# Second attention of a two-layer block: plain FP32 scores on 32 rows a head, in four row groups, for split scores on 64 rows that went by DRAM

## What is computed

```python
x = L0_attn_x
xn = _layernorm(x, axis=-1)
s = _L0_attn_ref(xn, ...); g = _silu(_L0_ffn_ref(xn, ...)); x = x + s * g
xn = _layernorm(x, axis=-1)
s = _L1_attn_ref(xn, ...)      # below
g = _silu(_L1_ffn_ref(xn, ...))
x = x + s * g

# _L1_attn_ref, HEADS = 16, HEAD_DIM = 16
Q, K, V = X @ Wq + bq, X @ Wk + bk, X @ Wv + bv
...
scores = jnp.einsum('bhqd,bhkd->bhqk', q, k) / np.sqrt(HEAD_DIM)
attn = jax.nn.softmax(scores, axis=-1)
out = jnp.einsum('bhqk,bhkd->bhqd', attn, v)
out = out.transpose(0, 3, 2, 1).reshape(b, s, HEADS * HEAD_DIM)
return out @ Wo + bo
# _L1_ffn_ref: gelu(x16 @ W0.T + bias0) in float16, then @ W1.T + bias1
```

## Time and profile before

| | |
|---|---|
| median of 3 runs | 925.28 us (924.87 to 926.04) |
| the profiled execution | 921.1 us, of which the span is 919.2 us |
| mean granted clock of TensorE | 0.955 of full speed |
| busy share of the span: TensorE, VectorE, ScalarE, GpSimd | 86%, 67%, 51%, 34% |

### The profile page before, as it was taken

One profiled execution on the slowest core, in us unless ns is written; L12 is line 12 of the kernel. 1 busy time (PEld: TensorE's weight loads), 2 busy tenths in 40 slices (PEclk: granted clock), 3 DMA queues, 4 the chain that ended last, 5 costly groups with the idle time before them and its releaser, 6 DMA issues.

```text
span 919.2 us, 13147 instructions
## 1 busy us (share of the span) xinstructions
PE 793.2 (86%) x4544; PEld 480.1 (52%) x4544; DVE 620.4 (67%) x1653; ACT 466.7 (51%) x948; POOL 313.8 (34%) x264
## 2 busy tenths in 40 slices
PE   3556497787999999997999999997999999987996
PEld 1334265673533666773533666773533666763533
DVE  3886757763985677673985677764986577753972
ACT  4456355423367667322467676232477676232464
POOL 0582857200200788200201888200201888100201
PEclk9876789899999999998999999999999999998999
DMA  7311001208300311008300311018200310018200
GB/s 238 114 31 36 23 1 47 75 0 214 86 1 13 94 52 31 1 22 215 63 3 19 88 52 30 1 42 214 45 3 25 81 30 1 1 39 213 49 3 23
DMA packets 54001, 53.25 MB, mean 58 GB/s; under 512 B 14512, under 2 KB 43568, under 8 KB 53936
## 3 DMA queue, kind: packets, MB, share of 16 engines
q1 hardware_dynamic: 51488, 49.70, 20.4%
q10 hardware_dynamic: 2128, 1.68, 0.6%
q0 software_dynamic: 320, 1.05, 0.4%
HBM read 39.00 MB, written 13.14 MB: 57 GB/s over the span
## 4 chain that ended last, share of the span: by engine, by line
PE 56%; DVE 11%; issue 9%; ACT 8%; POOL 7%; DMA 4%; SPq 3%; POOLq 0%; DVEq 0%; ACTq 0%
PE bank L882 9%; PE bank L987 6%; PE bank L976 5%; PE bank L916 5%; PE bank L1153 5%; PE bank L1141 5%; PE bank L1094 4%; PE bank L1126 3%; PE bank L1048 3%; DVE mx L1493 3%; POOL region L567 3%; PE bank L926 2%; PE bank L1131 2%; PE bank L1080 2%; PE bank L958 2%
## 5 line engine op out<-in xcount | busy, mean ns | idle before, releaser
L1493 DVE TENSOR_REDUCE mx<-bank 128x1 f32<-128x512 f32 x256 | 162.9, 683 | 78.8 <-PE bank L1094 77.8
L882 PE MATMUL bank<-xnT,wrope 128*128 128x512 f32 x320 | 151.1, 615 | 18.5 <-ACT region L712 10.4
L567 POOL TENSOR_TENSOR region<-region 128x512 f32<-128x512 f32 x80 | 106.2, 1327 | 175.4 <-DVE region L1328 170.7
L822 ACT ACTIVATE region<-bank 128x512 f32<-128x512 f32 x256 | 136.3, 597 | 52.5 <-PE bank L1131 48.9
L729 ACT ACTIVATE region<-region,nb 128x128 f32<-128x128 f32 x256 | 81.6, 390 | 97.9 <-DVE nb L1335 97.7
L600 POOL TENSOR_TENSOR region<-region,bo_bc 128x256 f32<-128x256 f32 x16 | 11.7, 729 | 289.0 <-DVE region L1384 289.0
L882 PEld LDWEIGHTS bank<-xnT,wrope 128*128 128x128 f32 x320 | 59.6, 197 | 81.2 <-issue 72.1
L1094 PE MATMUL bank<-Kp,Qp 64*128 64x512 f32 x256 | 68.1, 450 | 23.9 <-DMA Kp<-scratch 20.1
L563 POOL TENSOR_TENSOR region<-region,sin_sb 128x512 f32<-128x512 f32 x60 | 80.4, 1340 | 24.5 <-ACT region L712 23.9
L916 PE MATMUL bank<-region 128*128 128x128 f32 x512 | 75.8, 294 | 11.3 <-ACT region L724 9.7
L1321 DVE TENSOR_TENSOR region<-bank,cos_sb 128x512 f32<-128x512 f32 x80 | 54.7, 688 | 43.5 <-PE bank L882 43.3
(11 more groups left out here) (135 smaller groups left out, 1345.3 us busy)
## 6 DMA issues: line engine op xcount, KB each, us to landing
wrope<-in_wrope SPq DMA_DIRECT2D x80, 128.0 KB, 2.1
scratch<-region SPq DMA_DIRECT2D x32, 256.0 KB, 3.8
Qp<-scratch SPq DMA_DIRECT2D x64, 128.0 KB, 3.7
Kp<-scratch SPq DMA_DIRECT2D x64, 128.0 KB, 3.9
X<-in_x SPq DMA_DIRECT2D x4, 512.0 KB, 4.0
scratch<-region SPq DMA_DIRECT2D x16, 128.0 KB, 3.3
out<-X SPq DMA_DIRECT2D x16, 128.0 KB, 2.0
VW<-v_rows SPq DMA_DIRECT2D x16, 102.0 KB, 2.8
```

Source lines behind the costliest of these rows:

```text
L567: nc.gpsimd.tensor_tensor(dst, dst, tiles(sw[:, r % 2, :], i), ALU.add)\
L822: nc.scalar.activation(P1[:, n % 8, :], turned_bank(n)[:, :], ACT.Exp, scale=SCALE1)\
L882: mm = nc.tensor.matmul(misc(b, name)[:, 0:width], lhs(c), xnT[:, c, :], start=(c == 0), stop=(c == DC - 1))
L1493: nc.vector.tensor_reduce(mx1[:, g % 2, column:column + 1], s_ring[m % 3][:, :], AX.X, ALU.max)\
```

## The change

A head gets 32 rows: its 16 dimensions, and 16 rows of which the first is 1 in `Kp` and the negated maximum in `Qp`. The scores are plain FP32, nothing is split, and nothing goes by DRAM: `queries` on ScalarE and `keys` on VectorE write Q and K from PSUM to their rows, once for the even and once for the odd groups, with `own_rows` (1 or 0 for each row) as a factor. Four heads fill the four row groups of 32. The maxima's rows go into `Qp` itself, so the second matmul of a turned tile is gone. The lead holds 7 groups of 4 scores tiles over 4 banks, with one up job behind each (two behind the last); the down projections move to the main loop and the wide part, in portions of 4 to 12 matmuls (`DOWN_STEPS`, by pairs of turned tiles `q`). `down` and `mt` share one bank. In the main loop the four row groups of a half step are those of its two turned and its two scores tiles. `ffn_rows`, `gate_of` and the tanh move with the down projections.

```diff
-HALF = 4 * HD
-NPAIR = NH // 2
+ROWS = 2 * HD
 LEAD = 4 * GH + 12
 WIDE_FROM = 4 * NH - LEAD
-N_SPILL, N_DEAL = 6, 8
-UP_FIRST, DOWN_FROM, DOWN_STEP = 6, 3, 9
+QUADS = LEAD // GH
+UP_PER_QUAD = (1, 1, 1, 1, 1, 1, 2)
+MT_QUAD = 5
+DOWN_STEPS = {0: (0, 12), 1: (0, 12), **{q: (1, 4) for q in range(3, 9)}, **{q: (2, 4) for q in range(11, 17)},
+              **{q: (3, 8) for q in range(20, 26, 2)}}
...
-    jobs += [("dup", i) for i in range(HC)] + [("down", 0), ("down", 1), ("mt", 0), ("down", 2), ("down", 3)]
-    jobs += [("mt", g) for g in range(1, NG)]
+    jobs += [("dup", i) for i in range(MT_QUAD + 1)] + [("mt", 0)] + [("dup", i) for i in range(MT_QUAD + 1, HC)]
+    jobs += [("down", 0)] + [(kind, t) for t in range(1, TT) for kind in ("mt", "down")]
...
-PLACED = {"xh": (0,), "qk": (1, 2, 3, 4), "v1": (5, 6), "dup": (1, 2, 3, 4), "down": (3, 4, 1, 2), "mt": (2,)}
+PLACED = {"xh": (0,), "qk": (1, 2, 3, 4), "v1": (5, 6), "dup": (3, 4), "down": (2,), "mt": (2,)}
...
+TANHS = (7, 21, 37, 54)
+FFN_ROWS, GATES = (33, 47, 62), (38, 53)
...
+        s_quad = s_bank + m_bank[0:2]
+
+        def scores_bank(m):
+            return s_quad[m % 4] if m < LEAD else s_ring[(m - LEAD) % 3]
+
+        def scores_tile(m):
+
+            g, p, par = m // (4 * GH), m % (4 * GH) // 2, m % 2
+            return g, 2 * (1 - p % 2) + par, p // 2
 
         def turned_bank(n):
 
             if n < WIDE_FROM:
                 return t_ring[n % 3]
             k = (n - WIDE_FROM) % 6
-            return t_ring[k] if k < 3 else s_ring[(4 * NH - 6 + k) % 3]
+            return (t_ring + s_ring)[k]
...
-            def spill(b, half): ...
-            def deal(b, g): ...
             def max_rows(b, g):
 
...
-                for part, done in enumerate((mrhi_ready, mrlo_ready)):
...
+                sp.wait_ge(mr_ready.sem, mr_ready.at(b, g + 1))
+                for h in range(GH):
+                    row = h * ROWS + HD * (1 - g % 2)
+                    sp.dma_start(Qp[row:row + 1, g, :].rearrange("o (t c) -> o t c", c=P),
+                                 mr[h * TT:(h + 1) * TT, :]).then_inc(m_loaded[g % 2].sem, 16)
...
+            def queries(b, half):
+                misc_wait(act, b, ("qk", 2 * half))
+                src = misc(b, ("qk", 2 * half))[:, :].rearrange("p (q s) -> p q s", s=S16)
+                for odd in range(2):
+                    g = 2 * half + odd
+                    nc.scalar.activation(Qp[:, g, :].rearrange("p (s q) -> p q s", s=S16), src, ACT.Identity,
+                                         bias=bqk_sb[:, g:g + 1], scale=own_rows[:, odd:odd + 1])\
+                        .then_inc(q_ready.sem, 1)
...
+                def max_rows(g):
+                    misc_wait(act, b, ("mt", g))
+                    nc.scalar.activation(mr[:, :], misc(b, ("mt", g))[0:4 * GH, 0:P], ACT.Copy)\
+                        .then_inc(mr_ready.sem, 1)
...
+                    if i == MT_QUAD:
+                        max_rows(0)
...
                 for g in range(NG):
                     for i in range(4 * GH):
                         n = 4 * GH * g + i
                         act.wait_ge(t_full.sem, t_full.at(b, L0T + n + 1))
                         nc.scalar.activation(P1[:, n % 8, :], turned_bank(n)[:, :], ACT.Exp, scale=SCALE1)\
                             .then_inc(p1_ready.sem, 1)
                         if i == 5 and g + 1 < NG:
-                            max_high(g + 1)
+                            max_rows(g + 1)
+                        if n in TANHS:
+                            half_tanh1(TANHS.index(n))
...
+                    g, h, t = scores_tile(m)
+                    if m >= LEAD + 3:
                         pe.wait_ge(mx1_done.sem, mx1_done.at(b, m - 2))
+                    elif m >= 4:
+                        pe.wait_ge(mx1_done.sem, mx1_done.at(b, m - 3))
+                    elif m >= 2:
+                        pe.wait_ge(q_ready.sem, q_ready.at(b, 2))
                     else:
                         pe.wait_ge(v1_ready.sem, v1_ready.at(b, m + 1))
                     if m % (4 * GH) == 0:
+                        pe.wait_ge(q_ready.sem, q_ready.at(b, g + 1))
+                        pe.wait_ge(k_ready.sem, k_ready.at(b, g + 1))
+                    rows = slice(h * ROWS, (h + 1) * ROWS)
+                    nc.tensor.matmul(scores_bank(m)[:, :], Qp[rows, g, t * P:(t + 1) * P], Kp[rows, g, :],
+                                     start=True, stop=True).then_inc(s_full.sem, 1)
...
+                def scores_turned(n):
+
+                    g, k, h = n // (4 * GH), n // GH % TT, n % GH
+                    if n >= WIDE_FROM + 6:
+                        pe.wait_ge(p1_ready.sem, p1_ready.at(b, n - 5))
+                    elif n >= WIDE_FROM + 3:
+                        pe.wait_ge(mx1_done.sem, mx1_done.at(b, 4 * NH - 5 + n - WIDE_FROM))
+                    elif n >= 3:
+                        pe.wait_ge(p1_ready.sem, p1_ready.at(b, n - 2))
+                    elif n == 2:
+                        pe.wait_ge(mx1_done.sem, mx1_done.at(b, LEAD))
+                    else:
+                        pe.wait_ge(gelu_done.sem, gelu_done.at(b, HC - 1 + n))
+                    rows = slice(h * ROWS, (h + 1) * ROWS)
+                    nc.tensor.matmul(turned_bank(n)[:, :], Kp[rows, g, k * P:(k + 1) * P], Qp[rows, g, :],
+                                     start=True, stop=True).then_inc(t_full.sem, 1)
...
+                ups = iter(range(HC))
+                for quad in range(QUADS):
+                    for h in range(GH):
+                        scores1(GH * quad + h)
+                    for _ in range(UP_PER_QUAD[quad]):
+                        up1_job(next(ups))
+                    if quad == MT_QUAD:
                         turn_max(0)
...
+                def down_part(q):
+                    if q in DOWN_STEPS:
+                        t, count = DOWN_STEPS[q]
+                        first = sum(c for p, (j, c) in DOWN_STEPS.items() if j == t and p < q)
+                        if q == 0:
+                            pe.wait_ge(gelu_done.sem, gelu_done.at(b, HC))
+                        down(t, first, first + count)
 
                 for g in range(NG):
                     pe.wait_ge(m_loaded[g % 2].sem, m_loaded[g % 2].at(b, 64 * (g // 2) + 64))
                     for k in range(TT):
+                        n = 4 * GH * g + GH * k
+                        q = n // 2
+                        if n >= WIDE_FROM:
+                            for h in range(GH):
+                                scores_turned(n + h)
+                            if k == 1 and g + 1 < NG:
                                 turn_max(g + 1)
+                            down_part(q)
+                        else:
+                            for hp in range(2):
+                                for m in (n + 2 * hp, n + 2 * hp + 1):
+                                    scores_turned(m)
+                                for m in (n + 2 * hp, n + 2 * hp + 1):
+                                    scores1(m + LEAD)
+                                if (k, hp) == (1, 0):
+                                    turn_max(g + 1)
+                                down_part(q + hp)
                         if k or g:
                             attend1(g if k else g - 1, (k - 1) % TT)
...
+                def keys(half):
+                    misc_wait(dve, b, ("qk", 2 * half + 1))
+                    for odd in range(2):
+                        g = 2 * half + odd
+                        nc.vector.tensor_scalar(Kp[:, g, :], misc(b, ("qk", 2 * half + 1))[:, :],
+                                                own_rows[:, odd:odd + 1], bqk_sb[:, NG + g:NG + g + 1],
+                                                ALU.mult, ALU.add).then_inc(k_ready.sem, 1)
...
-                    if i == 2 and g:
-                        max_low(g - 1)
                     if m in FFN_ROWS:
                         ffn_rows(FFN_ROWS.index(m))
                     if m in GATES:
                         t = GATES.index(m)
                         gate_of(b, 1, t, e16[:, t, 0:DIM])
-                max_low(NG - 1)
+                gate_of(b, 1, 2, e16[:, 2, 0:DIM])
                 if b + 1 < B:
                     first_norm(b + 1)
+                ffn_rows(3)
                 outputs1(b, NG - 2)
+                gate_of(b, 1, 3, e16[:, 3, 0:DIM])
                 outputs1(b, NG - 1)
```

More of the change, by code:

```diff
@@ L178, in build @@
         rden = sb("rden", [P, S16])
[L179 to L182, removed]
+        Qp = sb("Qp", [P, NG, SEQ])
+        Kp = sb("Kp", [P, NG, SEQ])
         mx1 = sb("mx1", [P, 2, 4 * GH])
@@ L222, in build @@
         e16 = F.bitcast(F16)
-        mr = cut(6656, 2, P)[0:4 * GH].bitcast(F32R)
-        stage = [cut(at_, 2, 2, SEQ).bitcast(F32R) for at_ in (7680, 0)]
+        mr = cut(6656, P)[0:4 * GH]
         WCOL = 2 * HID * DIM // P + DIM * HID // P
@@ L428, in load_wrope @@
```

(34 more changed lines are left out.)

139 lines of the change are left out of this document (17 added, 122 removed).

## The result

The changed kernel takes 944.8 us (942.0 to 948.0), the one before 925.4 beside it: a ratio of 1.021, with an interval of 1.018 to 1.024. It is 19.5 us slower, where +26.7 was forecast. Its profiled execution takes 944.8 us too, with a span of 943.0; the profiled span of before was 919.2, so the two traces differ by 23.8 us.

The account below looks back on a forecast made before the run. TensorE, 56% of the waits' chain, was taken as the bound. Lead -11.1, main loop +12.7 and wide part +5.0 gave +6.6 us a batch, +26 for four: 947.5 profiled, 952 us as median, range 926 to 978.

Parts of the forecast that it names:

- The price of four FP32 tiles: Four FP32 tiles in four row groups: 1.09 us to the next job, 1.2 to the reader, priced from attend1.
- The rule of strict order: Skill's rule that matmuls start and end in order across tiles; one tile's second record would hold back the next's first.
- The lead: Second attention's opening: DRAM wait of 4.94 us goes, groups run 3.12 apart; 25.3 us long, -11.1 a batch.
- a lead that doesn't shrink: Rival: the DRAM wait goes, but bank ring and first group's wait for V take more; 4.0 a group, 976 us; chance 0.05.
- The main loop: Second attention's nine steps: ring of 4.01 us each plus down matmuls and waits; 42.4 against 29.7, +12.7 a batch.
- the sixth's term: Main loop, step 6: VectorE first makes a group's outputs and ffn_rows(1), so the maxima come late: +0.8 us.
- the first step: Main loop: two portions of 12 down matmuls add 2.0 us; one pushes the second half from 1.94 to 2.51.
- The wide part: Second attention's last part: seven steps of 2.07 us, down portions, a turning, waits and an end; 21.9 against 16.9, +5.0.
- the 2.0 of waits behind the tanhs: Wide part: some 2.0 us of waits for a bank behind the 0.4 us tanh that ScalarE now has there twice.
- Start and end: First batch's start loses three constant writes and gains a small load, beside the weights' loads; last tanh, gate, bias covered: nothing.
- Work alone: Rival: tiles come free before they are needed, main-loop step 3.16 us; -3.7 a batch, 910 us; chance 0.14.
- Row groups in turn: Rival: row groups run one behind the other, four tiles take 2.4 us instead of 1.09; +167, 1119 us; chance 0.08.

Follow-up runs that it names:

- experiment 5: The changed kernel with all scores matmuls on rows 0 to 31 for every head, so in one row group: 1665 us.
- experiment 3: The changed kernel with exp and maximum over 256 of a tile's 512 columns, TensorE's work the same: 911.8 us.

## Why the prediction was right

The direction, the mechanism and, within the range, the size were as forecast. By its own steps:

- **The price of four FP32 tiles**, 1.09 and 1.2: measured 1.07 and 1.15. The column groups of attend1 were a good stand-in. The rule of strict order of the Trainium skill, "TensorE: Matmul & The Clock Gate", Part 3, would put the scores tiles' first records behind the turned tiles' second; the trace shows the former at 254.97 and the latter at 255.49. The same part's 3.07 times gave 1.37 by my estimate; measured is 1.07, and against the one row group of experiment 5 it is 3.63 / 1.07 = 3.4 times.
- **The lead**, -11.1: measured -12.8. The pitch was right (3.12, measured 3.09). The second group started 3.6 after the lead's start instead of 4.0, and the rows landed 1.1 after their last issue (234.49 - 233.41) instead of 2.0. The rival of a lead that doesn't shrink wanted a pitch of 4.0 and is ruled out by this.
- **The main loop**, +12.7: measured +13.8 and +13.6 in two batches. The steps of 4.01 and 4.56 stood to 0.01, the second at 5.80 against 5.76, and the sixth's term was right within 0.15 in three batches (5.85 in the first, against 5.36). The last scores tile of a step starts at 1.99, 0.05 behind the 1.94 of the sum. Mis-sized was the first step, 5.03 by my terms and 5.53 to 5.67 in the trace: its second turned tile waits for the last gelu and starts 0.56 to 0.70 after the first, for which the sum had nothing, and the second half starts at 3.04 to 3.18 instead of 2.51. In the second and fourth batch another 1.5 us come from the stretch at 1.2 GHz behind the wait at `turn_max` (44.8 against the 43.3 of the third), a cost of a wait that the sum had no term for.
- **The wide part**, +5.0: measured +3.6. A portion of 8 costs 3.03 - 2.05 = 0.98, as priced. Of the 2.0 of waits behind the tanhs some 0.8 showed: two steps are 0.5 longer than the 2.05 of the others, the first of them with the turning's 0.2 in it.
- **Start and end**, "nothing": 0.8 for the small load, and 2 us for where the stretches at 1.2 GHz fall in the first layer and at the end.
- **Rivals.** Work alone: ruled out by experiment 3, since shorter readers shorten the step with the matmuls as they are. Row groups in turn: ruled out by the records and by experiment 5.

The errors of the three stages, -1.7, +1.7 and -1.4 a batch, came to -1.4, or -5.6 over four batches, and the 3 us outside gave half of that back. The lead's error and the main loop's, 7 us each over four batches, cancel by luck: they have different causes. Against the medians (+19.5, forecast +26.7) the error is 7 us, 4 of them because I carried the change over from a profiled execution that lay 4 us under its median.

## What to carry to other kernels

A way by DRAM that is on the path costs its wait once; matmuls of twice the passes cost theirs in every turn of a ring of banks, and the ring's length counts even where no reader is busy all the time. So price the ring, not the engines: matmul, reader, signal. And place work that moves (here the down projections) where the ring waits, in a first half or in the lead (0.08 us for a portion of 8, 1.3 for 48 matmuls): in a second half it costs its whole length (0.55 for 4). The way without the scratch paid once each tile was one record (unsplit FP32R, without the low part that the kernel before kept of Q and K): 0.943 of the time.

## What the hardware showed

- Four FP32 matmuls of 32 rows in four row groups run side by side in both their records: first records within 0.02 us for tiles of two different lines, second records 0.53 later, the next job 1.07 after the start. In one row group they take 3.63, and as FP32R, with one record each, 0.43 in four.
- A wait of TensorE costs twice when the granted clock falls behind it: 1.87 us at `turn_max` cost 1.2 us in the step, and in two of four batches 1.5 more. In the other two no stretch at 1.2 GHz followed the same wait, nor behind the 1.34 us of experiment 3.
- TensorE was granted 1.2 GHz also while busy without a gap, when all its tiles lay in one row group (experiment 5: 7.20 busy of 7.20, clock 0.50). The runs don't show why.
